# Attention gathers run first, and experts' rows are gated as they leave PSUM

## The reference

```
x = x + gnn(layernorm(x))          # three graph convolutions
x = x + ffn(layernorm(x)[None])    # four experts, the best two of each node

# ffn
h = (x_flat @ W_gat).reshape(M, HEADS, NUM_EXPERTS)        # 4 heads, 4 experts
e = leaky_relu(a_src[src] + a_dst[dst], negative_slope=0.2) # 131,072 edges and a loop per node
ee = exp(e - segment_max(e, dst)[dst])
alpha = ee / (segment_sum(ee, dst)[dst] + 1e-16)
agg = segment_sum(h[src] * alpha, dst) + b_gat
scores = layernorm(agg).reshape(M, HEADS, NUM_EXPERTS).mean(1)
topk_s, topk_i = top_k(scores, 2);  w = softmax(topk_s)
for ei in range(NUM_EXPERTS):
    g = where(topk_i == ei, w, 0.0).sum(-1)
    hh = gelu(x @ W1[ei] + b1[ei])                          # 256 -> 512
    out = out + g[..., None] * (hh @ W2[ei] + b2[ei])       # 512 -> 256
```

## Time and profile before

| | us |
|---|---|
| median of 3 runs | 8284.64 (8282.66 to 8292.05) |
| span of the profiled execution | 10,757.3 |
| of it, up to the last stage | 7843.8 |
| of it, experts beside attention gathers | 2543.3 |
| of it, from the first node gather to the end | 370.2 |
| TensorE busy, whole span | 2354.0 |
| VectorE busy | 3773.2 |
| GpSimd busy | 6413.3 |

### The profile page before, as it was taken

How to read it: one execution, slowest core, us unless ns; L and a number is a source line. 1 busy time by engine, 2 the same in 40 slices (tenths; PEclk the granted TensorE clock), 3 DMA queues, 4 the chain that set the end, 5 groups by cost and what they waited for, 6 DMA issues and landing times.

```text
span 10757.3 us, 49102 instructions
## 1 busy us (share of the span) xinstructions
PE 2354.0 (22%) x10310; PEld 1918.9 (18%) x10310; DVE 3773.2 (35%) x7766; ACT 1979.6 (18%) x3186; POOL 6413.3 (60%) x6399
## 2 busy tenths in 40 slices
PE   1122000000300000000300000000635556665664
PEld 0111000000300000000300000000524445554553
DVE  4556655543333333332333333333501111111125
ACT  1111111111411111111311111111301111111112
POOL 4655666676477777776477777776473443333343
PEclk9999999998655555555655555555857677777787
DMA  4444555555555555555555555555621111111126
GB/s 134 158 158 167 174 180 179 177 197 169 177 192 187 187 187 187 187 187 170 168 193 187 187 188 187 187 187 178 198 49 44 35 32 45 45 43 40 45 72 182
DMA packets 589401, 1573.35 MB, mean 146 GB/s; under 512 B 137512, under 2 KB 378388, under 8 KB 550484
## 3 DMA queue, kind: packets, MB, share of 16 engines
q1 hardware_dynamic: 302196, 877.99, 22.6%
q0 software_dynamic: 285488, 678.64, 21.9%
q10 hardware_dynamic: 1584, 15.48, 0.4%
HBM read 810.67 MB, written 760.96 MB: 146 GB/s over the span
## 4 chain that ended last, share of the span: by engine, by line
DVE 14%; PE 13%; another core or an unknown queue 11%; issue 11%; POOL 1%; DMA 1%; ACT 1%; SPq 0%; DVEq 0%; POOLq 0%; ACTq 0%
DVE ps L1215 12%; PE ps L1642 6%; PE ps L1653 6%; POOL acc L1083 1%; PE ps L1690 1%; DMA onehot<-feature_table 0%; ACT work L1705 0%; DVE work L1244 0%; DVE acc L1254 0%; PE ps L1165 0%; DVE stats L1260 0%; ACT acc L1768 0%; DMA x_normed_t<-keep_within_node 0%; DVE acc L2031 0%
## 5 line engine op out<-in xcount | busy, mean ns | idle before, releaser
L1083 POOL DMA_INDIRECT acc<-feature_table,staged_indices x4608 | 4689.0, 1018 | 2148.5 <-issue 1596.4
L1215 DVE SCALAR_TENSOR_TENSOR ps<-ps,keep_within_node,acc 128x256 f32<-128x256 f32 x4692 | 2310.1, 492 | 3589.7 <-DVE ps L1215 1432.6
L1545 POOL DMA_INDIRECT acc<-attention_table,idx x1024 | 986.2, 963 | 1445.5 <-DVEq L1841 1134.9
L1003 ACT COPY acc<-ps 128x1024 f32<-128x1024 f32 x787 | 796.9, 1013 | 3782.4 <-DVE ps L1215 3280.5
L1127 PE MATMUL ps<-work,carry_from_partition 128*128 128x256 f32 x4 | 2.4, 714 | 4400.9 <-ACT work L1003 4400.9
L1642 PE MATMUL ps<-work 128*128 128x256 f32 x3136 | 801.8, 401 | 706.1 <-issue 519.5
L1800 DVE TENSOR_TENSOR acc<-ps,acc 128x512 f32<-128x512 f32 x196 | 135.6, 692 | 2177.8 <-DMA onehot<-feature_table 1022.1
L1653 PE MATMUL ps<-work,onehot 128*128 128x256 f32 x3136 | 763.0, 391 | 345.2 <-issue 331.1
L1127 PEld LDWEIGHTS ps<-work,carry_from_partition 128*128 128x128 f32 x4 | 1.0, 311 | 4401.8 <-ACT work L1003 4401.8
L1642 PEld LDWEIGHTS ps<-work 128*128 128x128 f32 x3136 | 627.9, 201 | 855.2 <-issue 572.3
L1705 ACT ACTIVATE work<-ps,eb_sb 128x256 f32<-128x256 f32 x784 | 307.7, 475 | 2200.3 <-remote 1161.6
(11 more groups left out here) (393 smaller groups left out, 3020.1 us busy)
## 6 DMA issues: line engine op xcount, KB each, us to landing
unning_features_of_edges<-acc SPq DMA_DIRECT2D x195, 2048.0 KB
unning_features_of_edges<-work SPq DMA_DIRECT2D x96, 2048.0 KB
acc<-feature_table,staged_indices POOLq DMA_INDIRECT x4608
expert_rows<-acc SPq DMA_DIRECT2D x196, 256.0 KB
onehot<-feature_table SPq DMA_DIRECT2D x147, 256.0 KB
feature_table<-acc SPq DMA_DIRECT2D x98, 256.0 KB
acc<-attention_table,idx POOLq DMA_INDIRECT x1024
work<-expert_rows SPq DMA_DIRECT2D x14, 1024.0 KB
```

The source lines that it names most:

```text
L1003: nc.scalar.copy(sums_out[slot][:, 4 * j:4 * j + w].rearrange("p c f -> p (c f)"), ps[:, b:b + 2].rearrange("p a f -> p (a f)")[:, 0:w * D ...
L1083: nc.gpsimd.indirect_dma_start(out=rows_in[r][:, k], out_offset=None, in_=table, in_offset=bass.IndirectOffsetOnAxis(ap=staged[:, r, k:k + ...
L1215: nc.vector.scalar_tensor_tensor(state[k % HELD], state[(k - 1) % HELD if k else before], keep1[:, c + k:c + k + 1], rows_in[r][:, k], ALU ...
L1545: nc.gpsimd.indirect_dma_start(out=rows[:, i % 2, c], out_offset=None, in_=gat_table, in_offset=bass.IndirectOffsetOnAxis(ap=idx[1][:, sta ...
```

## The change

The order of the last stage is turned round.

- Eight pairs (HELD_PAIRS) are still evicted whole, stored, and read back. Six of them (EARLY, 24 experts) run during the attention gathers: EVICTED places three evictions ahead of each chunk, and a chunk's steps then follow one another without a break.
- After the last chunk come the joining of the ends, the node gathers, one eviction, and `route(0)`, now for 16 pairs at once; then the other seven evictions of the held pairs.
- The 41 pairs from 8 on are evicted by `add_gated`: VectorE adds the gated bias and the gated product, straight from PSUM, onto a tile that already holds x (ring_x, loaded by SyncE up to nine jobs ahead). The result is stored as the output. `route(1)`, for the other 33 pairs, is made in pieces after every second expert.
- A held pair is mixed by `add_held` behind each of the pairs 16 to 23, with eight scalar_tensor_tensor.
- Gone are the diagonals, the products with them, the copies, the gathers of chosen rows and what computes their indices. TensorE's loop covers pairs 9 to 48; pairs 0 to 8 are written out.

```diff
-        SPANS = ((0, 6), (6, 17), (17, 32), (32, PAIRS))
+        SPANS = ((0, 16), (16, PAIRS))
+        HELD_PAIRS, EARLY = 8, 6
+        EVICTED = (3, 6, 9, 12, 15, 18, 21, 23, 23)
...
-                for x in range(NE):
-                    pool.wait_ge(s_yo[x], 16 * PAIRS)
-                for g in range(PAIRS):
-                    if chosen_rows(g):
...
-                for g in range(PAIRS):
+                for g in range(HELD_PAIRS):
+                    if g == EARLY:
+                        sp.wait_ge(s_run, NC)
+                        for n in range(SLOTS):
+                            load_x1(n)
...
+                load_held(0)
+                load_held(1)
+                done = 0
+                for g in range(HELD_PAIRS, PAIRS):
+                    if g + 1 < PAIRS:
+                        sp.wait_ge(s_up, g * NE)
+                        load(g + 1)
+                    while done < job_of[g]:
+                        store(done)
+                        done += 1
+                store(done)
...
+                held_freed = lambda g, x: (s_yc, g * NE + (x + 1))
+                gated_freed = lambda g, x: (s_acc, g * (4 * NE) + (4 * x - 4 - HELD_PAIRS * NE * 4))
...
+                def evict_held(n):
+                    g, x = n // NE, n % NE
+                    if g >= 1:
+                        dve.wait_ge(s_yo[x], 16 * g)
+                    dve.wait_ge(s_dn, n + 1)
+                    nc.vector.tensor_tensor(yst[:, x], ps[:, 4 + x % 2].rearrange("p (a f) -> p a f", a=2),
+                                            b2[:, x].unsqueeze(1).broadcast_to([P, 2, D]), ALU.add).then_inc(s_yc, 1)
+
+                def add_gated(g, x):
+                    n = job_of[g]
+                    r = n % SLOTS
+                    added = ((g - HELD_PAIRS) * NE + x) * 4
+                    if x == 0:
+                        dve.wait_ge(s_xin[r], 16 * (n // SLOTS + 1))
+                    for step, of in enumerate((lambda a: b2[:, x], lambda a: ps[:, 4 + x % 2, a * D:(a + 1) * D])):
+                        if step == 1:
+                            dve.wait_ge(s_dn, g * NE + x + 1)
+                        for a in range(2):
+                            if x > 0 or step > 0:
+                                dve.wait_ge(s_acc, added + 2 * step + a - 1)
+                            nc.vector.scalar_tensor_tensor(ring_x[:, r, a], of(a), gates[:, g * 2 + a, x:x + 1], ring_x[:, r, a],
+                                                           ALU.mult, ALU.add).then_inc(s_acc, 1)
...
+                begun = 0
+                for i in range(NC):
+                    for n in range(begun, EVICTED[i] + 1):
+                        evict_held(n)
+                    begun = EVICTED[i] + 1
...
+                    for _ in chunk(i):
+                        pass
+                ends_of_partitions()
+                scan_ends()
+                carry_ends()
+                fix_rows()
...
-                groups = [route(q) for q in range(len(SPANS))]
-                for _ in groups[0]:
+                evict_held(EARLY * NE)
+                for _ in route(0):
                     pass
...
+                for n in range(EARLY * NE + 1, HELD_PAIRS * NE):
+                    evict_held(n)
+                rest = route(1)
+                for g in range(HELD_PAIRS, PAIRS):
+                    for x in range(NE):
+                        add_gated(g, x)
+                        if x % 2:
+                            next(rest, None)
+                    if not jobs[min(job_of[g] + 1, PAIRS - 1)][1]:
+                        add_held(jobs[job_of[g] + 1][0])
```

More of the change, by code:

```diff
@@ L1447, in build @@
         fix_t = area(2, CH)
-        x1t = area(2, 2, D)
         assert at[0] <= NB * D
         SLOTS = 9
-        SPANS = ((0, 6), (6, 17), (17, 32), (32, PAIRS))
[L1452 to L1458, removed]
+        SPANS = ((0, 16), (16, PAIRS))
+        HELD_PAIRS, EARLY = 8, 6
+        EVICTED = (3, 6, 9, 12, 15, 18, 21, 23, 23)
+        assert len(EVICTED) == NC and EVICTED[-1] == EARLY * NE - 1
+        jobs = []
+        for g in range(HELD_PAIRS, PAIRS):
+            jobs.append((g, True))
+            if 0 <= g - SPANS[0][1] < HELD_PAIRS:
+                jobs.append((g - SPANS[0][1], False))
+        job_of = {pair: n for n, (pair, _) in enumerate(jobs)}
+        assert len(jobs) == PAIRS and HELD_PAIRS <= SPANS[0][1]
         group_of = lambda g: sum(g >= g1 for _, g1 in SPANS)
+        SLOTS = 9
         slot = 2 * NE * D
@@ L1644, in down, with body @@
                     mm.then_inc(s_dn, 1)
-                def body(g, r, uses, beside=lambda x: None):
+                def body(g, r, uses, freed):
                     pe.wait_ge(s_xt[r], uses * 16)
@@ L1682, in _ @@
[L1682 to L1692 removed]
+                            down(g, x - 1, freed(g, x - 1))
@@ new lines, in body @@
+                    down(g, NE - 1, freed(g, NE - 1))
+                held_freed = lambda g, x: (s_yc, g * NE + (x + 1))
+                gated_freed = lambda g, x: (s_acc, g * (4 * NE) + (4 * x - 4 - HELD_PAIRS * NE * 4))
+                for g in range(EARLY):
+                    body(g, g % 2, g // 2 + 1, held_freed)
+                pe.wait_ge(s_tail, 1)
+                for j in range(3):
+                    mm = nc.tensor.transpose(ps[0:CH, 6, j * P:(j + 1) * P], tails[:, j], ident[:])
@@ L1694, in _ @@
+                assert (PAIRS - g0 - 1) % 2 == 0 and g0 % 2 == 0
+                with pe.Fori(0, (PAIRS - g0 - 1) // 2) as q:
+                    for j in range(2):
+                        body(q * 2 + (g0 + 1 + j), (g0 + 1 + j) % 2, q + ((g0 + 1 + j) // 2 + 1), gated_freed)
             @block.scalar
@@ L1783, in _ @@
+                act.wait_ge(s_put, 16 * NB)
+                act.dma_start(first_rows, first_dram[0:E2].rearrange("(p c) f -> p c f", p=P)).then_inc(s_first, 16)
+                for g in range(PAIRS):
+                    pair(g, between)
+                for r in range(2):
+                    act.wait_ge(s_out[r], 16 * turns[r])
             @block.vector
```

297 lines of the change are left out of this document (81 added, 216 removed).

## The result

The changed kernel takes 9226.58 us (four runs, 9221.14 to 9230.91) against 8283.87 (four runs, 8282.66 to 8292.05): a ratio of 1.1135, 95% interval 1.1121 to 1.1149. The forecast was 9207 us.

A forecast was written before the change was run, and what follows sets the result against it. TensorE's 1354 us of experts, overlapping the gathers, bounds the last stage. Un-interleaving makes it 1249 + 28 + 41 + 25 + 41 + 1133 + 14 = 2531 us against 1609, +922: 9207 us, 8 in 10 within 8950 to 9300.

The forecast's parts named there:

- The sum that gave the time: Last stage and tail, without the stall: 1609 us before, 2531 after, so +922 us on the median of 8285.
- c: Spacing of GpSimd's gathers, taken as 1.22 us, midway between the trace's 1.25 and the fitted 1.19.
- The fit: Whole kernel before, engines overlapping: 4693 layer gathers plus 1100 plus 1609 us; 1.19 us per gather gives 8294.
- Stall or overlap: Whether TensorE stalls beside the last stage's gathers in timed runs; overlap chosen, needing a 5% correction against 20%.
- The rest of the 2473 us I put down to what recording the execution adds: Gap between profiled span 10,757.3 us and median 8284.64, attributed to recording beyond the slower gather spacing; called inference.
- a span of 10,820 us: Changed kernel's profiled execution, whole span: nearly unchanged at about 10,820 us (10,700 to 10,950) while time grows 11%.
- The first rival: Last stage: stall as real in timed runs as in the trace; 8251 us, 0.4% faster; chance 0.08.
- The sum made against the profile's own time: Last stage and tail with the stall on both sides: 2978 us after against 2913.5 before.
- The second: Rival on the last stage: half of the stall is real, giving 8729 us; chance 0.06.
- The third: Rival in the gated pairs: VectorE's eviction makes TensorE wait, +82 us at most, 9290 us; chance 0.08.
- a queue 16 deep: Bursts of attention gathers: something drains at 1.40 us per gather, 16 gathers deep; when full, all engines queue.

The follow-up runs named there:

- the paced kernel: Kernel before with two chained memsets ahead of each attention gather: 8645.17 us against 8286.36 (ratio 1.0434) without the stall; 9922.34 against 10,773.26 (0.9200) on a stalling chip.

## Why the prediction was right, and where it was not

**The sum that gave the time.** By its own terms, from the changed kernel's trace, predicted and measured: the gathers 1249 and 1286 us (6669.5 to 7955.2); from there to the first node gather 28 and 25; the node gathers up to the gates 41 and 41 (to 8021.41); the gates 25 and 26 (to 8047.47); the six held experts and 41 pairs 41 + 1133 = 1174 and 1169 (to 9216.7); the end 14 and 11. Together 2531 and 2558. The stage before: 1609 and 1621. The difference: +922 and +938, and on the medians +943. Both stages came out longer than their sums, by 27 and 12 us, so a part of the error cancels.

**The term that was mis-sized is c**, the spacing of gathers: 1.22 was taken, halfway to a fitted 1.19, and it is 1.25 to 1.26 as the trace before had it. Of the +27 us of the stage after, the gathers are +37. The fit went wrong since it put all of the difference to 8285 on the gathers and kept 1100 us for what lies outside them in the layers. In the changed kernel's trace those parts are 758 us (6669.5 less 1974.6, 1970.0 and 1966.9). They, too, were stretched in the profile before. At c = 1.22 the prediction's own sum for the kernel before is 5726 + 1100 + 1609 = 8435 us, 150 over the median; the forecast added only the difference of the stages to the median, so this did not reach it.

**Stall or overlap.** Overlap was right for the timed runs, and it was argued from a sum although every row of the trace of before spoke against it. That step held: 1621 us leave no room for a stall. But luck has a part in the result. The median before told which state the runs before were in; that the changed kernel would be timed in the same state, and not as on three of the four chips met later, nothing in the prediction secured. There the same forecast would have been wrong in size and in sign.

**"The rest of the 2473 us I put down to what recording the execution adds": this step failed.** Recording adds nothing that shows: time and span differ by 1.7 to 2.0 us in executions of either kind (9229.94 and 9227.9; 10,741.25 and 10,739.5; 10,775.18 and 10,773.5). The gap was between two kinds of chip. With it fell the forecast of a span of 10,820 us beside a time of 9207: the span came out at 9228, the time itself. The text took the two numbers for one state with and without a recorder; they were two states.

The Trainium skill (Runtime: NRT & Kernel Launch, The launch sequence) gives a gap of some 6.2 us between a profile's total and the reported time, whatever the kernel, and the prediction said that the measurement decides against it. In these runs the gap is 1.7 to 2.0 us and lies the other way: the reported time is longer than the span, where the Trainium skill has the profile's total the longer. But the rule's sense, a small constant gap, holds within one execution, and the prediction was wrong to set it aside. That the timed runs stall too, which the prediction drew from the rule as a rival, follows only where the times and the profile come from one state. The Trainium skill says that interleaving regimes may pay (Perfetto Trace Analysis, Optimization Strategy). The runs without the stall agree (un-interleaving costs 943 us), those under it do not (64 experts interleaved save nothing).

**The first rival**, a stall as real as in the trace, gave 0.4% faster. On the stalling chip that ran both kernels the ratio is 0.9906, 0.9% faster: its mechanism and sign were right there, though its price took gathers 1.00 us apart, which no run shows. The sum made against the profile's own time said +64 us and the runs say -101. It erred in the gathers' phase, 1610 for 1505 us, by charging all but the first chunks at 1.40 us and 25 us of catching up behind each: less the 24 experts at 7.3, a gather there cost 1.3 us. **The second**, half of the stall, has little for it: but for one run of 9083 us (below), each run of the whole kernels is of one kind or the other. **The third**, the eviction as the longer leg, is refuted by the trace: pairs 27.62 us apart, TensorE busy 1111.0 of 1111.0 us.

**What stays open.** What differs between the chips; they were not chosen, the instructions are the same on all, and whether the state can come and go within one chip is not known: of the kernel before's seven runs on the chip without the stall six took 8285 to 8292 us and one 9083 at a lower mean clock (0.666, the others 0.745 to 0.747). Which part of the path it is that empties at 1.40 us, when the DMA engines are busy for 0.01 of the time behind a burst; and its depth: at 1.34 us a gather, 16 gathers put it less than 1 us behind, and TensorE was starved after 20 us all the same (from 8407.8), so the picture of a queue 16 deep that must first fill does not hold in detail. And, on a chip without the stall, the dose of cover (24 held pairs), which would have shown the cause of the +943 by a second point; it rests on the traces' account above, whose terms each agree within 5 us but for the gathers, and on the overlap in the paced kernel's trace.

## What to carry to other kernels

Before a profile is used to price a change, put its span beside the time of its own execution: when they agree and the other runs do not, the profile shows another state of the machine, and every duration of it has to be asked whether it belongs to the state that is timed. Work hidden beside a long serial stretch of gathers is worth its full length when both really run side by side, and nothing when the gathers back up, so the same reordering can be an 11% loss and a 1% gain. Where gathers back up, spacing them out a little was worth more here (8.0%) than moving work around them (0.9%).

## What the runs showed of the hardware

- The same program takes 8286 us (median) on one chip and 10,739 to 10,775 on three others. The difference is in how GpSimd's gathers bear on the other engines: 1970 against 2194 us for 1565 feature gathers, and 1621 against 2923 us for the last stage and its tail.
- A stalling chip takes gathers 1.59 us apart with no effect on TensorE (stage 1679.6 against 1682.0 us), and at 1.34 leaves it 99 matmuls in 144.6 us, a seventh of the 680 of full pace. Slowing GpSimd made the kernel 8.0% faster.
- The stall outlasts a burst in proportion to it: it ends 88.8 us after the start of 64 gathers and 179.8 us after the start of 128, 1.39 and 1.40 us for each.
- Two chained memsets of 0.22 us lengthened the spacing of gathers from 1.25 to 1.59 us, where 0.44 would have made 1.69, and one to 1.34: part of the 0.30 us of idle time ahead of a gather is not lost when other work stands there.
